# Gate/up products over three PSUM bank pairs, W_in loaded in two DMAs, and tile 1's transposes released per bank: a recurrent block with a gated MLP on eight Trainium2 cores

## The chip, the cores and the metric

The kernel runs on all 8 NeuronCores of one Trainium2 chip. The time of a run is the device time of the slowest core, in microseconds (us). The figure that is compared is the median of several runs. A profile is one more execution, recorded by the hardware profiler; its page shows the slowest core.

## What is computed

A layer norm feeds two branches: a linear recurrence along the sequence between two projections, and a gated MLP with integer weights scaled by 1/127. The result is x + s * silu(ffn).

```python
xn = layernorm(x)                       # x: (2, 16384, 1024) float32
# recurrent branch, on sequences of length 16384
gu = gamma * (xn @ W_in.T + b_in)
h[t] = lam * h[t-1] + gu[t]             # lam = exp(lambda_log), elementwise
s  = h @ W_out.T + b_out + xn
# gated MLP: DIM 1024, HIDDEN 3072, weights are int * (1/127)
g  = silu( (silu(xn @ wg.T) * (xn @ wu.T)) @ wd.T )
out = x + s * g
```

## The kernel before

Each core takes 4096 rows of one sequence (a quarter) in 8 tiles of 512 rows, numbered 1 to 8. Ahead of them stands tile 0, the 256 rows before the core's own, of which only the recurrence's state is wanted. The kernel is written for the five engines directly: `tensor_tile`, `scalar_tile`, `vector_tile`, `sync_tile` and `gpsimd_tile` each append one engine's instructions and waits for a tile, in the order in which that engine will run them. A wait (`W`) names a mark, and a mark is a semaphore's value once the operation (`O`) that carries it has ended. Nothing reorders: an engine that waits holds back all that stands behind it. DMAs issued by SyncE form the queue q1, those issued by GpSimd the queue q0.

TensorE runs these stages on a tile k:

- **T**: 8 blocks of 4 transposes (2 in tile 0) of the normalized rows `xnb` into PSUM banks 0 to 3, in turn (L245). Even blocks are copied to `xnbT` by ScalarE (L364), odd ones by VectorE (L418); the marks are `("Tevac", k, kc)`.
- **U**: 8 blocks of 8 matmuls with `winT` into banks 0 and 1 (L264). ScalarE scales them into `guT` (L379, marks `("guevac", k, ec)`), and VectorE scans them (L425).
- **gate/up**, not in tile 0: 24 blocks c of 8 gate matmuls (L287) and 8 up matmuls (L295). Their weights come in 12 groups of two blocks, 1 MB each, through two buffers `wgubuf`; SyncE reloads one (L504) when the up matmuls of the group two before are done. ScalarE applies SiLU to the gate bank (L390, marks `gsilu`), VectorE multiplies it with the up bank (L458, marks `gumul`) into `hbT`, and runs one scan after each third block. There are two `siluT` buffers.
- **S**: 8 blocks of one bias matmul (L310) and 8 matmuls with `woutT` (L315) into banks 0 and 1, evacuated by VectorE (L471).
- **down**: 4 row blocks m, in the order 1, 0, 2, 3, of 48 matmuls each with `wdfull` (L333), into banks 2m and 2m+1. ScalarE applies SiLU to each bank (L348, marks `("dsilu", k, b)`); for the banks 4 to 7 it does so after the next tile's T stage. GpSimd multiplies with s and adds x (L527, L531), and stores (L542).

In the gate/up stage a block uses two pairs of banks in turn:

```python
gb = 2 + 2 * (c % 2)
ub = 3 + 2 * (c % 2)
if c >= 2:
    W("tensor", mark=("gsilu", k, c - 2))
    W("tensor", mark=("gumul", k, c - 2))
```

At the start, SyncE issues x for tile 0 in two halves (L145), three small loads (eps, lambda, the identity) between them, x for tile 1 (2 MB, L139), five more small loads (gamma, b_in, b_out, mask, ones; L156), and then the first two `wgubuf` groups. GpSimd issues `winT` as one DMA that casts float32 to bf16 (L160), waits for it (L162), and then issues `woutT` (L165), the four parts of `wdfull` (L513) and x for tile 2 (L139). TensorE starts with two waits: for the three and for the five small loads (L169, L170). VectorE likewise waits for the five before it takes the statistics of tile 1 (L185), and ScalarE takes their square root (L210) before it evacuates tile 0's transposes. ScalarE normalizes tile 1 (L226) between those evacuations and the first evacuation of tile 0's U stage.

Of the kernel before, what the change touches and what calls it, by code (L numbers as in the profile page):

```python
# [63 lines left out]
def build_nc():  # L64
# [65 lines left out]
    def walk():  # L130
# [23 lines left out]
        for src, dst in ((gam_h, gam_sb), (bin_h, bin_sb), (bout_h, bout_sb),  # L154
                         (mask_h, mask_sb), (ones_h, ones_sb)):
            O("sync", lambda eng, s=src, d=dst: eng.dma_start(d[:, :], s[:, :]),  # L156
              inc="s_sets", n=16)
        src_w = win_t.rearrange("(kc p) e -> p kc e", p=128)
        dst_w = winT[:, :].rearrange("p (kc e) -> p kc e", e=D)
        O("gpsimd", lambda eng, s=src_w, d=dst_w: eng.dma_start(d, s),  # L160
          inc="s_setg", n=16, mark=("wcast", 0))
        W("gpsimd", mark=("wcast", 0))  # L162
        src_w2 = wout_t.rearrange("(kc p) e -> p kc e", p=128)
        dst_w2 = woutT[:, :].rearrange("p (kc e) -> p kc e", e=D)
        O("gpsimd", lambda eng, s=src_w2, d=dst_w2: eng.dma_start(d, s),  # L165
          inc="s_setg", n=16, mark=("wcast", 1))


# [64 lines left out]
        def tensor_tile(k):  # L233
            real = k >= 1
            W("tensor", mark=("LN", k))
            if k == 1:
                W("tensor", mark=("guevac", 0, 7))
            jw = 2 if k == 0 else 4
            for kc in range(NK):
                if kc >= 4:  # L240
                    W("tensor", mark=("Tevac", k, kc - 4))
                elif k >= 2:
                    W("tensor", mark=("dsilu", k - 1, kc))
                for j in range(jw):
                    O("tensor", lambda eng, kc=kc, j=j: eng.transpose(  # L245
                        pb[kc % 4][:, j * 128:(j + 1) * 128],
                        xnb[:, j * D + kc * 128: j * D + kc * 128 + 128],
                        ident_sb[:, :]),
                        inc=None if j < jw - 1 else "s_t",
                        mark=None if j < jw - 1 else ("T", k, kc))  # L250
            if k == 0:
                W("tensor", mark=("wcast", 0))
            for ec in range(NK):
# [7 lines left out]
                for kc in range(NK):  # L261
                    if ec == 0:
                        W("tensor", mark=("Tevac", k, kc))
                    O("tensor", lambda eng, ec=ec, kc=kc, tw=tw: eng.matmul(  # L264
                        pb[ec % 2][:, 0:tw],
                        winT[:, kc * D + ec * 128: kc * D + ec * 128 + 128],
                        xnbT[:, kc * T: kc * T + tw],
                        start=(kc == 0), stop=(kc == NK - 1)),
                        inc=None if kc < NK - 1 else "s_t",
                        mark=None if kc < NK - 1 else ("U", k, ec))  # L270
            if not real:
                return
            for g in range(NGU):
                G = (k - 1) * NGU + g
                W("tensor", mark=("wgu", G))
                for cc in range(2):
                    c = 2 * g + cc
                    gb = 2 + 2 * (c % 2)
                    ub = 3 + 2 * (c % 2)
                    if c >= 2:  # L280
                        W("tensor", mark=("gsilu", k, c - 2))
                        W("tensor", mark=("gumul", k, c - 2))
                    elif k >= 2:
                        W("tensor", "s_a",
                          mark=("dsilu", k - 1, 3 if c == 0 else 5))
                    for kc in range(NK):
# [65 lines left out]
        def scalar_tile(k):  # L352
# [33 lines left out]
            for c in range(NHC):  # L386
                W("scalar", mark=("gmm", k, c))
                if c >= 2:
                    W("scalar", mark=("gumul", k, c - 2))
                O("scalar", lambda eng, c=c: eng.activation(  # L390
                    siluT[c % 2][:, :], pb[2 + 2 * (c % 2)][:, 0:512],
                    AF.Silu, scale=QINV),
# [8 lines left out]
        def vector_tile(k):  # L401
# [53 lines left out]
            for c in range(NHC):  # L455
                W("vector", mark=("umm", k, c))
                W("vector", mark=("gsilu", k, c))
                O("vector", lambda eng, c=c: eng.scalar_tensor_tensor(  # L458
                    hbT[:, c * T:(c + 1) * T], pb[3 + 2 * (c % 2)][:, 0:512],
                    QINV, siluT[c % 2][:, :], ALU.mult, ALU.mult),  # L460
# [205 lines left out]
```

How the kernel before makes its waits and increments, by code:

```python
    def play(eng, name):  # L575
        for item in sc.ops[name]:
            if item[0] == "op":
                _, make, inc, n = item
                ins = make(eng)
                if inc is not None:
                    ins.then_inc(sems[inc], n)
            else:
                _, sem, v = item
                eng.wait_ge(sems[sem], v)
```

## Time and profile before

| | |
|---|---|
| median of 2 runs | 1372.91 us (1371.90 to 1373.91) |
| the profiled execution | 1371.94 us |
| its span on core 0, the slowest | 1370.4 us |
| spans of all cores | 1355.9 to 1370.4 us |
| TensorE matmul busy on core 0 | 1294.2 us, 94% |
| VectorE, ScalarE, GpSimd busy | 347.0, 289.9, 198.9 us |
| DMA | 190.90 MB |
| granted TensorE clock | 0.992 to 0.995 |

The span runs from the first to the last instruction of a core. Busy times are sums over instructions; a TensorE that is 94% busy has few gaps, so what matters is where these gaps lie and what ends them. All times below count from the start of core 0's span.

### The profile page before, as it was taken

What the parts mean: (1) busy time and instruction counts of PE and PEld (TensorE: products, weight loads), DVE (VectorE), ACT (ScalarE), POOL (GpSimd) and SP (SyncE); (2) the same over time, 40 slices, a digit from 0 to 9 for tenths busy, and PEclk for the clock granted to TensorE, in tenths of its full rate; (3) what the DMA queues carried; (4) which work ended last, traced back from release to release, by engine and by line L of the source; (5) the groups of instructions that cost most, each with busy time, mean ns of one, the idle gap of its engine ahead of it and who ended that gap; (6) DMA issues with size and microseconds to landing.
All of it is one profiled execution on the core that took longest, in us unless ns stands there. A gap on an engine that the chain in (4) does not pass through costs nothing.

```text
span 1370.4 us, 15875 instructions; the slowest of 8 cores (1355.9 to 1370.4 us)
## 1 busy us (share of the span) xinstructions
PE 1294.2 (94%) x6032; PEld 588.9 (43%) x6032; DVE 347.0 (25%) x566; ACT 289.9 (21%) x437; POOL 198.9 (15%) x197
## 2 busy tenths in 40 slices
PE   0699999999998999989999899999999999999997
PEld 0444445444453445434454344544445444454443
DVE  1423321223112240123301233022320334012322
ACT  2521123110231112311222112221123110231100
POOL 0000021300312003210042001330031300331002
PEclk9999999999999999999999999999999999999999
DMA  9954405753067410865127640366306652065301
GB/s 209 249 159 154 123 16 176 220 173 93 31 215 219 150 62 31 261 200 153 32 62 248 203 150 14 112 229 213 123 19 189 220 160 90 31 220 178 124 1 62
DMA packets 124782, 190.90 MB, mean 139 GB/s; under 512 B 3491, under 2 KB 101923, under 8 KB 124708
## 3 DMA queue, kind: packets, MB, share of 16 engines
q1 hardware_dynamic: 101524, 103.90, 24.5%
q0 software_dynamic: 23184, 85.99, 20.2%
q8 instruction: 50, 0.82, 0.2%
q14 instruction: 24, 0.20, 0.1%
HBM read 177.29 MB, written 16.78 MB: 142 GB/s over the span
## 4 chain that ended last, share of the span: by engine, by line
PE 87%; DMA 10%; issue 1%; DVE 1%; ACT 0%; SPq 0%; ACTq 0%; DVEq 0%; POOL 0%; POOLq 0%
PE pb L333 24%; PE pb L287 21%; PE pb L295 21%; PE pb L315 9%; PE pb L264 9%; DMA wgubuf<-wgu_t 8%; PE pb L245 2%; DMA ones_sb<-ones 2%; PE pb L310 1%; DVE stats L185 0%; ACT xnb L226 0%; SPq L156 0%; ACT guT L379 0%; DVE xbuf L486 0%; ACT L230 0%
## 5 line engine op out<-in xcount | busy, mean ns | idle before, releaser
L287 PE MATMUL pb<-xnbT,wgubuf 128*128 128x512 bf16 x1536 | 367.0, 383 | 24.9 <-DMA wgubuf<-wgu_t 23.1
L295 PE MATMUL pb<-xnbT,wgubuf 128*128 128x512 bf16 x1536 | 363.7, 380 | 0.0
L333 PE MATMUL pb<-wdfull,hbT 128*128 128x512 bf16 x1536 | 332.8, 379 | 0.0
L458 DVE SCALAR_TENSOR_TENSOR hbT<-pb,siluT 128x512 bf16<-128x512 f32 x192 | 132.8, 692 | 597.7 <-PE pb L295 597.7
L287 PEld LDWEIGHTS pb<-xnbT,wgubuf 128*128 128x128 bf16 x1536 | 149.0, 98 | 214.4 <-issue 41.1
L390 ACT ACTIVATE siluT<-pb 128x512 bf16<-128x512 f32 x192 | 114.6, 597 | 567.3 <-PE pb L287 561.1
L295 PEld LDWEIGHTS pb<-xnbT,wgubuf 128*128 128x128 bf16 x1536 | 150.5, 98 | 182.8 <-issue 2.6
L333 PEld LDWEIGHTS pb<-wdfull,hbT 128*128 128x128 bf16 x1536 | 150.1, 98 | 181.4
L527 POOL TENSOR_TENSOR gslab<-gslab,s_sb 128x512 bf16<-128x512 bf16 x60 | 70.9, 1181 | 812.5 <-ACT gslab L348 805.4
L264 PE MATMUL pb<-xnbT,winT 128*128 128x512 bf16 (+1 forms) x576 | 122.1, 374 | 4.0 <-ACT guT L379 4.0
L315 PE MATMUL pb<-woutT,guT 128*128 128x512 bf16 x512 | 121.6, 381 | 0.0
L531 POOL TENSOR_TENSOR xbuf<-xbuf,gslab 128x512 f32<-128x512 f32 x60 | 74.8, 1247 | 180.0 <-issue 176.0
L264 PEld LDWEIGHTS pb<-xnbT,winT 128*128 128x128 bf16 x576 | 57.5, 100 | 65.4 <-issue 4.7
L418 DVE CAST xnbT<-pb 128x512 bf16<-128x512 f32 (+1 forms) x36 | 23.6, 662 | 242.9 <-PE pb L245 242.7
L425 DVE TENSOR_TENSOR_SCAN guT<-lam_sb,carry,guT 128x512 bf16<-128x512 f32 x64 | 82.7, 1292 | 0.0
L245 PE MATMUL pb<-ident_sb,xnb 128*128 128x128 f32 x272 | 33.8, 282 | 39.4 <-DMA ones_sb<-ones 32.5
L315 PEld LDWEIGHTS pb<-woutT,guT 128*128 128x128 bf16 x512 | 44.8, 98 | 59.9 <-issue 14.5
L379 ACT ACTIVATE guT<-pb,bgam_sb,gam_sb 128x512 bf16<-128x512 f32 (+1 forms) x72 | 54.4, 756 | 57.1 <-PE pb L264 57.1
L471 DVE TENSOR_TENSOR s_sb<-pb,xnb 128x512 bf16<-128x512 f32 x64 | 44.3, 692 | 87.5 <-PE pb L315 87.5
L348 ACT ACTIVATE gslab<-pb 128x512 bf16<-128x512 f32 x64 | 33.9, 601 | 91.4 <-PE pb L333 66.3
L210 ACT ACT_TABLE_LOAD x9 | 11.5, 1283 | 194.9 <-DVE mv L190 194.9
L364 ACT CAST xnbT<-pb 128x512 bf16<-128x512 f32 (+1 forms) x36 | 20.1, 561 | 149.9 <-PE pb L245 149.9
(29 smaller groups left out, 242.4 us busy)
## 6 DMA issues: line engine op xcount, KB each, us to landing
wgubuf<-wgu_t SPq DMA_DIRECT2D x96, 1024.0 KB, 5.8
wdfull<-wd_t POOLq DMA_DIRECT2D x32, 1536.0 KB, 18.7
out<-xbuf POOLq DMA_DIRECT2D x32, 512.0 KB, 3.0
xbuf<-xe POOLq DMA_DIRECT2D x7, 2048.0 KB, 13.1
winT<-win_t POOLq DMA_DIRECT2D x1, 2048.0 KB, 30.3
xbuf<-xe SPq DMA_DIRECT2D x1, 2048.0 KB, 26.0
woutT<-wout_t POOLq DMA_DIRECT2D x1, 2048.0 KB, 18.8
xbuf<-xe SPq DMA_DIRECT2D x2, 512.0 KB, 8.6
```

The lines of the kernel that those rows point to most:

```text
L245: O("tensor", lambda eng, kc=kc, j=j: eng.transpose(pb[kc % 4][:, j * 128:(j + 1) * 128], xnb[:, j * D + kc * 128: j * D + kc * 128 + 128] ...
L264: O("tensor", lambda eng, ec=ec, kc=kc, tw=tw: eng.matmul(pb[ec % 2][:, 0:tw], winT[:, kc * D + ec * 128: kc * D + ec * 128 + 128], xnbT[: ...
L287: O("tensor", lambda eng, g=g, cc=cc, kc=kc, gb=gb: eng.matmul(pb[gb][:, 0:512], wgubuf[g % 2][:, kc * 512 + cc * 128: kc * 512 + cc * 128 ...
L295: O("tensor", lambda eng, g=g, cc=cc, kc=kc, ub=ub: eng.matmul(pb[ub][:, 0:512], wgubuf[g % 2][:, kc * 512 + 256 + cc * 128: kc * 512 + 25 ...
L315: O("tensor", lambda eng, b=b, m=m, n=n, kc=kc: eng.matmul(pb[b % 2][:, 0:512], hTb[:, kc * T + m * 128: kc * T + m * 128 + 128], woutT[:, ...
L333: O("tensor", lambda eng, c=c, m=m, n=n: eng.matmul(pb[2 * m + n][:, 0:512], hbT[:, c * T + m * 128: c * T + m * 128 + 128], wdfull[:, c * ...
L379: O("scalar", lambda eng, ec=ec, tw=tw: eng.activation(guT[:, ec * T: ec * T + tw], pb[ec % 2][:, 0:tw], AF.Identity, bias=bgam_sb[:, ec:e ...
L390: O("scalar", lambda eng, c=c: eng.activation(siluT[c % 2][:, :], pb[2 + 2 * (c % 2)][:, 0:512], AF.Silu, scale=QINV), inc="s_a", mark=("g ...
L425: eng.tensor_tensor_scan(hTb[:, ec * T: ec * T + tw], lam_sb[:, ec:ec + 1].broadcast_to([128, tw]), guT[:, ec * T: ec * T + tw], init, ALU ...
L458: O("vector", lambda eng, c=c: eng.scalar_tensor_tensor(hbT[:, c * T:(c + 1) * T], pb[3 + 2 * (c % 2)][:, 0:512], QINV, siluT[c % 2][:, :] ...
L527: O("gpsimd", lambda eng, b=b, m=m, n=n: eng.tensor_mul(gslab[b % 4][:, :], gslab[b % 4][:, :], s_sb[:, m * D + n * 512: m * D + n * 512 + ...
L531: O("gpsimd", lambda eng, b=b, m=m, n=n, p=p: eng.tensor_add(xbuf[p][:, m * D + n * 512: m * D + n * 512 + 512], xbuf[p][:, m * D + n * 51 ...
```

## The change

In words: `winT` comes in two DMAs of four k-blocks each, and GpSimd waits for each before it issues the next; TensorE waits for a half when the first U block of tile 0 reaches it, instead of for all of it before the stage. TensorE's wait ahead of tile 1's transposes for the last evacuation of tile 0 becomes two waits, one per bank. The gate/up blocks use three pairs of banks (2 to 7) in turn instead of two (2 to 5), and wait for block c - 3 instead of c - 2; the third block of a tile waits for the SiLU of the last down bank of the tile before.

```diff
--- before.py
+++ after.py
@@ -155,15 +155,19 @@
                          (mask_h, mask_sb), (ones_h, ones_sb)):
             O("sync", lambda eng, s=src, d=dst: eng.dma_start(d[:, :], s[:, :]),
               inc="s_sets", n=16)
-        src_w = win_t.rearrange("(kc p) e -> p kc e", p=128)
-        dst_w = winT[:, :].rearrange("p (kc e) -> p kc e", e=D)
-        O("gpsimd", lambda eng, s=src_w, d=dst_w: eng.dma_start(d, s),
-          inc="s_setg", n=16, mark=("wcast", 0))
-        W("gpsimd", mark=("wcast", 0))
+        for h in range(2):
+            src_w = win_t[h * 512:(h + 1) * 512, :].rearrange(
+                "(kc p) e -> p kc e", p=128)
+            dst_w = winT[:, h * 4 * D:(h + 1) * 4 * D].rearrange(
+                "p (kc e) -> p kc e", e=D)
+            O("gpsimd", lambda eng, s=src_w, d=dst_w: eng.dma_start(d, s),
+              inc="s_setg", n=16, mark=("winh", h))
+            W("gpsimd", mark=("winh", h))
         src_w2 = wout_t.rearrange("(kc p) e -> p kc e", p=128)
         dst_w2 = woutT[:, :].rearrange("p (kc e) -> p kc e", e=D)
         O("gpsimd", lambda eng, s=src_w2, d=dst_w2: eng.dma_start(d, s),
           inc="s_setg", n=16, mark=("wcast", 1))
+
 
 
         W("tensor", "s_seta", value=NSETUP_A)
@@ -233,14 +237,14 @@
         def tensor_tile(k):
             real = k >= 1
             W("tensor", mark=("LN", k))
-            if k == 1:
-                W("tensor", mark=("guevac", 0, 7))
             jw = 2 if k == 0 else 4
             for kc in range(NK):
                 if kc >= 4:
                     W("tensor", mark=("Tevac", k, kc - 4))
                 elif k >= 2:
                     W("tensor", mark=("dsilu", k - 1, kc))
+                elif k == 1 and kc < 2:
+                    W("tensor", mark=("guevac", 0, 6 + kc))
                 for j in range(jw):
                     O("tensor", lambda eng, kc=kc, j=j: eng.transpose(
                         pb[kc % 4][:, j * 128:(j + 1) * 128],
@@ -248,8 +252,6 @@
                         ident_sb[:, :]),
                         inc=None if j < jw - 1 else "s_t",
                         mark=None if j < jw - 1 else ("T", k, kc))
-            if k == 0:
-                W("tensor", mark=("wcast", 0))
             for ec in range(NK):
                 if ec == 0:
                     W("tensor", mark=("Tevac", k, 4))
@@ -261,6 +263,8 @@
                 for kc in range(NK):
                     if ec == 0:
                         W("tensor", mark=("Tevac", k, kc))
+                        if k == 0:
+                            W("tensor", mark=("winh", kc // 4))
                     O("tensor", lambda eng, ec=ec, kc=kc, tw=tw: eng.matmul(
                         pb[ec % 2][:, 0:tw],
                         winT[:, kc * D + ec * 128: kc * D + ec * 128 + 128],
@@ -275,14 +279,14 @@
                 W("tensor", mark=("wgu", G))
                 for cc in range(2):
                     c = 2 * g + cc
-                    gb = 2 + 2 * (c % 2)
-                    ub = 3 + 2 * (c % 2)
-                    if c >= 2:
-                        W("tensor", mark=("gsilu", k, c - 2))
-                        W("tensor", mark=("gumul", k, c - 2))
+                    gb = 2 + 2 * (c % 3)
+                    ub = 3 + 2 * (c % 3)
+                    if c >= 3:
+                        W("tensor", mark=("gsilu", k, c - 3))
+                        W("tensor", mark=("gumul", k, c - 3))
                     elif k >= 2:
                         W("tensor", "s_a",
-                          mark=("dsilu", k - 1, 3 if c == 0 else 5))
+                          mark=("dsilu", k - 1, 3 + 2 * c))
                     for kc in range(NK):
                         O("tensor", lambda eng, g=g, cc=cc, kc=kc, gb=gb: eng.matmul(
                             pb[gb][:, 0:512],
@@ -388,7 +392,7 @@
                 if c >= 2:
                     W("scalar", mark=("gumul", k, c - 2))
                 O("scalar", lambda eng, c=c: eng.activation(
-                    siluT[c % 2][:, :], pb[2 + 2 * (c % 2)][:, 0:512],
+                    siluT[c % 2][:, :], pb[2 + 2 * (c % 3)][:, 0:512],
                     AF.Silu, scale=QINV),
                     inc="s_a", mark=("gsilu", k, c))
             if k < NT:
@@ -456,7 +460,7 @@
                 W("vector", mark=("umm", k, c))
                 W("vector", mark=("gsilu", k, c))
                 O("vector", lambda eng, c=c: eng.scalar_tensor_tensor(
-                    hbT[:, c * T:(c + 1) * T], pb[3 + 2 * (c % 2)][:, 0:512],
+                    hbT[:, c * T:(c + 1) * T], pb[3 + 2 * (c % 3)][:, 0:512],
                     QINV, siluT[c % 2][:, :], ALU.mult, ALU.mult),
                     inc="s_v", mark=("gumul", k, c))
                 if c % 3 == 1:
```

## Rows read from the trace of the kernel before

**Rows 1.** Cores: span and mean granted clock.
```profile
core 0: 1370.4 us, clock 0.993
...
core 6: 1366.6 us, clock 0.992
```
**Rows 2.** Waits of TensorE, core 0: line, releaser: total us, times, longest us.
```profile
PE pb L245 <- DMA ones_sb<-ones: 32.5, 1, 32.5
PE pb L287 <- DMA wgubuf<-wgu_t: 23.1, 17, 2.8
PE pb L245 <- ACT xnbT L364: 5.8, 1, 5.8
PE pb L264 <- ACT guT L379: 4.0, 2, 3.7
PE pb L287 <- DVE hbT L458: 0.9, 1, 0.9
```
**Rows 3.** Timeline, 16 to 33 us: start, us, what, count [idle before <-releaser].
```profile
16.00 1.29 DVE L185 BATCH_NORM_STATS2 stats<-xbuf 128x6 f32<-128x512 f32 x2 [9.36 <-DMA xbuf<-xe]
...
32.36 0.17 DVE L406 TENSOR_TENSOR bgam_sb<-bin_sb,gam_sb 128x8 f32<-128x8 f32 x1 [12.51 <-DMA ones_sb<-ones]
32.44 0.89 POOL L165 DMA_DIRECT2D woutT<-wout_t  x1 [29.81 <-DMA winT<-win_t]
```
**Rows 4.** Timeline, 42 to 62 us.
```profile
42.19 3.34 PE L264 MATMUL pb<-xnbT,winT 128*128 128x256 bf16 x16
...
49.24 5.92 PE L264 MATMUL pb<-xnbT,winT 128*128 128x256 bf16 x40 [3.71 <-ACT guT L379]
...
57.24 2.38 PE L245 MATMUL pb<-ident_sb,xnb 128*128 128x128 f32 x20 [0.81 <-ACT guT L379]
...
59.10 1.29 DVE L418 CAST xnbT<-pb 128x512 bf16<-128x512 f32 x2 [0.21 <-issue]
...
59.94 1.50 PE L245 MATMUL pb<-ident_sb,xnb 128*128 128x128 f32 x12 [0.32 <-DVE xnbT L418]
```
**Rows 5.** DMA queues (packets, MB, share): 0:16.5, 5:9, 14:25, 29.5:32, 35:36, 37:47 us.
```profile
q0 software_dynamic: 544, 1.11, 54.9%
...
q0 software_dynamic: 203, 0.42, 91.5%
...
q0 software_dynamic: 421, 0.86, 52.5%
q1 hardware_dynamic: 421, 1.70, 48.6%
...
q0 software_dynamic: 10, 0.01, 3.2%
...
q0 software_dynamic: 11, 0.02, 38.8%
...
q0 software_dynamic: 760, 1.56, 107.1%
```
**Rows 6.** DMA queues, 765:769 us, and the matmuls that waited (timeline).
```profile
q0 software_dynamic: 284, 1.16, 100.6%
...
775.73 3.47 PE L287 MATMUL pb<-xnbT,wgubuf 128*128 128x512 bf16 x8 [2.79 <-DMA wgubuf<-wgu_t]
```
**Rows 7.** Issue of x(2) (timeline); DMA issues, us to landing; first use of woutT.
```profile
36.60 0.79 POOL L139 DMA_DIRECT2D xbuf<-xe  x1
...
xbuf<-xe POOLq DMA_DIRECT2D x1, 2048.0 KB, 40.4
...
159.39 1.90 PE L315 MATMUL pb<-woutT,guT 128*128 128x512 bf16 x8
```
**Rows 8.** Timeline, tile 3: a product and the bank wait put down to it.
```profile
431.97 0.69 DVE L458 SCALAR_TENSOR_TENSOR hbT<-pb,siluT 128x512 bf16<-128x512 f32 x1 [1.57 <-PE pb L295]
...
436.13 1.89 PE L287 MATMUL pb<-xnbT,wgubuf 128*128 128x512 bf16 x8 [0.89 <-DVE hbT L458]
```
**Rows 9.** Timeline of ScalarE, tile 2: SiLU of the last four down banks.
```profile
221.41 2.07 ACT L348 ACTIVATE gslab<-pb 128x512 bf16<-128x512 f32 x4
```

## The prediction

> **What bounds the kernel now.** I read the cores first: the slowest, core 0, spans 1370.4 us, core 6 is next at 1366.6 [rows 1]. The profiled run took 1371.94 us, so 1.54 us lie around the span; the median of the two timed runs is 1372.91, 0.97 above it. My sum is made against 1371.94 and moved by +0.97 at the end.
>
> TensorE's waits come next [rows 2], since TensorE is busy for 94% of the span. Three parts count: 32.5 us before its first instruction, put down to the DMA of ones_sb; 5.8 and 4.0 us on ScalarE in the prologue; and 23.1 us in 17 waits for wgubuf reloads. One single wait, 0.9 us, is put down to the VectorE product that frees a gate/up bank. Whatever the change gives has to come from the prologue or from one of these named waits.
>
> The prologue is a chain behind one event. At 32.3 us the last small constant lands; VectorE goes on at 32.36 [rows 3], TensorE at 32.5. VectorE then does the statistics for tile 1, ScalarE waits for them before it evacuates tile 0's transposes (the 5.8 us), and TensorE reaches the first winT matmul at 42.19 [rows 4]. winT had landed when GpSimd went on, at 32.44 [rows 3], nearly 10 us before: the old wait for all of winT costs nothing.
>
> **Part 1, winT in two DMAs, with finer waits on TensorE.** By itself the finer wait is worth nothing, for the reason just given. What can move is when the constants land, because they share the DMA engines with winT. The two landings coincide within 0.1 us [rows 3], and from 29.5 to 32 us the queue of winT, q0, has only 10 packets left at 3.2% of 16 engines, about half of one engine [rows 5]: one last engine, shared by both queues, ends both.
>
> Now the split. q0 had moved 544 of winT's 1024 packets by 16.5 us; between 14 and 25 us it moved 421, or 38 per us [rows 5]. So half of winT (512) is moved at 16.5 - 32/38 = 15.7 us on average. The whole would be through at 16.5 + 480/38 = 29.1, while the last engine ends at 32.3, some 3 us late; half of that late at half way puts the landing of the first half at about 17.2. GpSimd sees it and issues the second. The nearest row for the hole that opens in q0 is woutT: issued at 32.44 [rows 3], its first 11 packets in 35 to 36 us at 38.8% [rows 5], so about 2.9 us from issue to packets. The second half starts at about 20.1.
>
> On the last engine, 17.2 to 32.3 are 15.1 us, half of them (7.5) for each queue. In the hole q1 has the engine alone and does 2.9 of its 7.5 us; 4.6 are left at 20.1, with 7.5 of q0.
> - If both then share equally, q1 ends after 9.2 us, at 29.3 to 29.4: the chain starts 2.9 us earlier. That is the good end.
> - If q0 first keeps the engine for itself for more than 2.9 us, all of winT is again moved before the constants; the engine's work is the same as before and they land at 32.3: gain 0.
>
> Which? Two rows speak for the second. When winT started, q0 had 91.5% of the engines from 5 to 9 us [rows 5], although x0's second half had been issued before, at 2.92; its statistics could start only at 16.00 [rows 3]. And from 765 to 769 us an x load of q0 had 100.6% while a wgubuf reload was pending, for which TensorE waited until 775.73 [rows 6]. By 9 us some 16 packets for each of 16 engines were through (203, and a few before 5 us) [rows 5]. 16 of the 32 that an engine has in a half cost 16/32 x 7.5 = 3.8 us on the last engine, more than 2.9. So I take a point near the zero end, **0.5 us saved**, for holds that turn out shorter. Both ends, 0 and 2.9, stay in the range.
>
> On who gets an engine the Trainium skill ("DMA: Bandwidth & Descriptors", section Queues, rings and completion order) says that each DMA engine turns to the next queue only after a whole packet of some 9 to 17 descriptors, at most 64. The trace agrees at the starts of q0's transfers (91.5% and 100.6%); by that rule the gain is the same 0 that the rows gave.
>
> The other effects of the split are covered. At the good end the second half has 7.5 - 4.6 = 2.9 us of work left at 29.3 and shares with wgubuf, so it lands at 35.1; it is first needed after the transposes, at 42.19 - 2.9 = 39.3: 4.2 us of cover. And the tile-0 projection stops after two blocks for 3.71 us until ScalarE comes back from tile 1's layer norm (49.24) [rows 4], so only a landing after about 43 costs anything, one for one from there. Queued behind GpSimd's two waits are woutT, four wdfull loads and last x(2), all later by at most 2.9 us. The last, x(2), landed at 36.6 + 40.4 = 77.0; woutT is first read at 159.39, and wdfull and x(2) after that [rows 7]: 79 us of cover at least. SyncE's queue waits for none of it.
>
> **Part 2, tile 1's first transposes.** Before, they wait for the last evacuation of tile 0 (0.81 us idle before 57.24) [rows 4]. After, block 0 can start when the projection ends, about 56.45, and block 1 waits for that last evacuation. But block 5 needs bank 1 back from VectorE, whose copy stands behind the last scan, the 8 carry copies and the mask product, and starts at 59.10 whatever TensorE does; TensorE waits for it before 59.94 [rows 4]. So the 0.8 us turn into a longer wait there: **0**, at most 0.8 if VectorE were not late.
>
> **Part 3, three pairs of gate/up banks.** The only bank wait on core 0 is 0.9 us before 436.13. The product that frees that bank (block 8, freeing it for block 10) ran from 431.97 for 0.69 us, so it had been done for 3.5 us [rows 8]. Block 10 is the first of a group, and what really came last was its wgubuf load, which a third pair doesn't touch. Normally the 8 matmuls of a half block take at most 1.89 us [rows 8], so a block between leaves over 3 us for a product of 0.69 (2.0 with a scan ahead): two pairs suffice. **0**, at most 0.9. The new wait, of block 2 for the SiLU of the last down bank, is covered: on tile 2 that group of four ran from 221.41 for 2.07 us [rows 9], ahead of every evacuation of U on the same engine, and U's 64 matmuls stand between them and the gate/up stage. siluT still has two buffers, so ScalarE's and VectorE's own waits stay.
>
> **Sum.** 1371.94 - 0.5 + 0 + 0 = 1371.4 on the profiled run's scale, 1372.4 on that of the median.
>
> **The rivals.**
> - *Equal sharing* of the second half with q1: 1372.9 - 2.9 = 1370.0. For it: 421 against 421 packets from 14 to 25 us [rows 5]. Against it: the first 5 us of winT and the x load at 765. Chance 0.27.
> - *A slow start of the second half* (the other side). From 5 to 9 us q0 moved 203 packets at 91.5%, 55 per us of a full share, while woutT alone moved 760 in 10 us at 107.1%, 71 [rows 5]. If each start of such a transfer has its first 256 packets at the slower rate, that is 256/55 - 256/71 = 1.1 us more engine work ahead of the constants; it decides once q0 also keeps the engines for over 2.9 us. Time 1372.9 + 1.1 = 1374.0. Against it: the x load's start moved 284 packets in 4 us, 71 per us [rows 6]. Chance 0.13.
> - *The wgubuf waits fall otherwise.* Core 0 waits 23.1 us for them [rows 2]. If a small shift re-deals how reloads meet x loads and stores, core 0 could lose up to the distance to the next core, 3.8 us [rows 1]: 1369.1; or some core could gain as much. Chance 0.10 for both together.
> - *The change removes waits of its own*: earlier transposes and the third pair give both their bounds, 0.8 + 0.9 = 1.7 us: 1371.2. [rows 4, 8] speak against both. Chance 0.05.
> - The forecast, 1372.4: chance 0.45.
>
> For one DMA more, the same page of the Trainium skill (section Anatomy of one DMA) gives a fixed cost of about 2.0 us; the hole read from woutT is 2.9 us from issue to first packet. With 2.0 the equal-sharing rival would be worth an estimated 2.0 us.
>
> **How the numbers follow.** The low end is equal sharing plus both bounds of parts 2 and 3, 1370.0 - 0.8 - 0.9 = 1368.3, less 1.0 for half the spread of the two timed runs: 1367.3. The high end is the slow start, 1374.0, plus 2.5, most of the 3.8 us by which a core could gain wgubuf waits: 1376.5. A change of over 2%, about what a measurement of this kernel can tell, is 27 us. No case here comes near it: winT's second half would have to land 27 us after 43, or more than all wgubuf waits (23.1) to vanish. Faster 0.01, within 2% 0.98, slower 0.01.
>
> **What would show it.** Right: TensorE's first wait still 31.5 to 32.5 us on core 0; q1's share falling under 20% for some us after about 20; the transposes of tile 1 starting earlier, but its projection at the old distance from the first instruction; the wgubuf waits as long as before in sum, with a bank wait now and then still named at the first block of a group. Equal sharing: first wait near 29.6. Wrong in its ground: a wait of TensorE on winT's second half, or gaps inside a wgubuf group that were there before and are gone.

## The result

The changed kernel takes 1364.32 us (median of 32 runs) against 1373.38 us (31 runs of the kernel before beside it). The ratio is 0.9936, 95% interval 0.9920 to 0.9953: 8.8 us faster, 0.64%, within 2%. The forecast was 1372.4 us with a range down to 1367.3, so the time lies 3 us below the range. It moved the way that was forecast, but by 9 us instead of 0.5. The ratios, and the mean spans below, are taken over the executions in which neither die ran at a lowered clock.

The profiled execution took 1361.88 us, 10 us less than the one of before. First two rows of the view of its cores (span, mean granted clock):

```profile
core 0: 1354.7 us, clock 0.994
...
core 6: 1360.4 us, clock 0.993
```

Then its page (of core 6, the slowest), the engines' busy time and the DMA issues (op, count, KB each, median us to landing):

```profile
PE 1293.2 (95%) x6032; PEld 590.3 (43%) x6032; DVE 347.9 (26%) x566; ACT 290.0 (21%) x437; POOL 197.0 (14%) x198
...
winT<-win_t POOLq DMA_DIRECT2D x2, 1024.0 KB, 16.1
xbuf<-xe SPq DMA_DIRECT2D x1, 2048.0 KB, 20.2
```

TensorE is as busy as before (1294.2 us then). The load of tile 1's x by SyncE takes 20.2 us to land; on the page of before it was 26.0. Now TensorE's waits on core 0 (line, releaser: total us, times, longest us), to be held against [rows 2]:

```profile
PE pb L249 <- DMA ones_sb<-ones: 23.7, 1, 23.7
PE pb L291 <- DMA wgubuf<-wgu_t: 16.4, 9, 3.8
PE pb L249 <- ACT xnbT L368: 5.8, 1, 5.8
PE pb L268 <- ACT guT L383: 3.6, 2, 3.4
...
PE pb L291 <- DVE hbT L462: 0.9, 1, 0.9
```

The first wait has gone from 32.5 to 23.7 us. It is the same on every core: 30.0 to 33.2 us before, 23.3 to 25.2 after. The other two waits of the prologue in the list, for ScalarE (ACT), are as long as they were, within 0.4 us. The following table holds means over the 8 cores, from the same two profiles; the first gate/up block is where the prologue ends for this purpose.

| mean over the cores, us | before | after |
|---|---|---|
| TensorE's first instruction | 31.52 | 23.98 |
| from there to tile 1's projection | 29.47 | 29.45 |
| start of the first gate/up block | 74.75 | 67.20 |
| from there to the end of the span | 1288.1 | 1287.6 |
| span | 1362.9 | 1354.8 |

7.5 of the 8.1 us in the mean span are gained before TensorE's first instruction. The timeline of the start on core 0 shows what was released when (start us, us, engine, line, what [idle before <-releaser]):

```profile
17.74 0.76 POOL L163 DMA_DIRECT2D winT<-win_t  x1 [15.26 <-DMA winT<-win_t]
...
23.54 0.17 DVE L410 TENSOR_TENSOR bgam_sb<-bin_sb,gam_sb 128x8 f32<-128x8 f32 x1 [4.59 <-DMA ones_sb<-ones]
...
33.36 3.62 PE L268 MATMUL pb<-xnbT,winT 128*128 128x256 bf16 x16
...
33.67 0.88 POOL L168 DMA_DIRECT2D woutT<-wout_t  x1 [15.18 <-DMA winT<-win_t]
```

GpSimd goes on behind the first half of winT at 17.7 us, the constants are in at 23.5 (before: 32.3, [rows 3]), and GpSimd goes on behind the second half at 33.7. By the trace the halves had landed some 0.5 us before that, at 17.2 and 33.1. And the DMA queues of the same core, in the stretches 5:9, 16:22, 22:23, 23:24 and 24:29 us (packets, MB, share of 16 engines):

```profile
q0 software_dynamic: 218, 0.45, 96.9%
q1 hardware_dynamic: 90, 0.04, 6.5%
...
q1 hardware_dynamic: 758, 1.72, 96.9%
q0 software_dynamic: 8, 0.01, 1.0%
...
q1 hardware_dynamic: 407, 0.25, 81.5%
q0 software_dynamic: 22, 0.05, 28.1%
...
q0 software_dynamic: 63, 0.13, 73.7%
q1 hardware_dynamic: 105, 0.11, 34.9%
...
q0 software_dynamic: 316, 0.65, 80.6%
q1 hardware_dynamic: 313, 0.32, 25.6%
```

Up to 9 us it is the picture of before [rows 5]. Then, from 16 to 22 us, q1 has 97% of the engines where it had about half. It puts x(1) and the small loads through in that time. The second half of winT was issued at 17.74, but its first packet comes at 21.95; from 23 us on it takes 74 to 81% of the engines, and by 23.5 the constants are in. From the landing of the first half to that packet are 4.8 us, where the forecast had 2.9, and q0 as a whole moves only 8 packets in the 6 us from 16 to 22.

### The profile page after: what moved, and what is told of

It is laid out like the page before. It is cut to its first block, busy times and chain, and to the rows that moved or that the text cites. A ratio compares the mean times of both kernels' runs of the same rounds, so it can differ in the third digit from the quotient of the medians.

```text
span 1360.4 us, 15876 instructions; the slowest of 8 cores (1345.2 to 1360.4 us)
## 1 busy us (share of the span) xinstructions
PE 1293.2 (95%) x6032; PEld 590.3 (43%) x6032; DVE 347.9 (26%) x566; ACT 290.0 (21%) x437; POOL 197.0 (14%) x198
## 4 chain that ended last, share of the span: by engine, by line
PE 90%; DMA 7%; DVE 1%; issue 1%; ACT 0%; SPq 0%; ACTq 0%; DVEq 0%; POOL 0%; POOLq 0%
PE pb L337 24%; PE pb L291 23%; PE pb L299 22%; PE pb L268 9%; PE pb L319 9%; DMA wgubuf<-wgu_t 5%; PE pb L249 2%; PE pb L314 1%; DMA ones_sb<-ones 1%; DVE stats L189 0%; SPq L156 0%; ACT xnb L230 0%; DVE hbT L462 0%; ACT guT L383 0%; DVE xbuf L490 0%
## 5 line engine op out<-in xcount | busy, mean ns | idle before, releaser
L291 PE MATMUL pb<-xnbT,wgubuf 128*128 128x512 bf16 x1536 | 365.8, 381 | 23.9 <-DMA wgubuf<-wgu_t 18.3
L422 DVE CAST xnbT<-pb 128x512 bf16<-128x512 f32 (+1 forms) x36 | 23.6, 661 | 242.9 <-PE pb L249 242.6
L249 PE MATMUL pb<-ident_sb,xnb 128*128 128x128 f32 x272 | 33.9, 282 | 31.3 <-DMA ones_sb<-ones 24.4
L368 ACT CAST xnbT<-pb 128x512 bf16<-128x512 f32 (+1 forms) x36 | 20.1, 562 | 150.0 <-PE pb L249 150.0
## 6 DMA issues: line engine op xcount, KB each, us to landing
xbuf<-xe SPq DMA_DIRECT2D x1, 2048.0 KB, 20.2
```

What stands on the lines that cost most here:

```text
L249: O("tensor", lambda eng, kc=kc, j=j: eng.transpose(pb[kc % 4][:, j * 128:(j + 1) * 128], xnb[:, j * D + kc * 128: j * D + kc * 128 + 128] ...
L291: O("tensor", lambda eng, g=g, cc=cc, kc=kc, gb=gb: eng.matmul(pb[gb][:, 0:512], wgubuf[g % 2][:, kc * 512 + cc * 128: kc * 512 + cc * 128 ...
```

## The experiments

The kernels e1 to e4 ran on one chip, e5 to e8 on a second, e9 to e12 on a third and e13 to e16 on a fourth, each group beside the kernel before on the same chip. The slowest of eight cores scatters by some 4 us from run to run, so beside the ratio I give the mean span over the cores, in the mean over the runs, as the difference from the kernel before, with its standard error (se); and from each kernel's profile TensorE's first instruction and the first gate/up block, in the mean over the cores. Only the second and the third chip have a profile of the unchanged kernel beside the others (e5, e10).

| kernel | ratio, 95% interval | mean span, against before, us | first instr. | first gate/up |
|---|---|---|---|---|
| winT split only (e1) | 0.9958 (0.9932 to 0.9984) | -7.0 (se 0.9) | 23.9 | 67.1 |
| the two other parts (e2) | 0.9983 (0.9956 to 1.0010) | -2.3 (0.7) | 30.7 | 73.8 |
| both halves at once (e3) | 0.9965 (0.9943 to 0.9986) | -2.5 (0.8) | 30.6 | 73.5 |
| small loads first (e4) | 0.9988 (0.9959 to 1.0017) | -0.6 (0.8) | 27.9 | 73.0 |
| before, control (e5) | 1.0002 (0.9973 to 1.0031) | +0.3 (1.1) | 31.2 | 74.6 |
| the changed kernel again (e6) | 0.9956 (0.9930 to 0.9982) | -7.7 (0.7) | 24.0 | 67.4 |
| winT late (e7) | 0.9969 (0.9941 to 0.9996) | -6.7 (0.8) | 22.0 | 64.9 |
| late, small loads first (e8) | 0.9988 (0.9949 to 1.0026) | -5.4 (1.2) | 16.6 | 62.4 |
| three bank pairs only (e9) | 0.9981 (0.9955 to 1.0007) | -1.5 (0.9) | 31.2 | 74.5 |
| before, control (e10) | 0.9987 (0.9957 to 1.0018) | -0.6 (1.1) | 30.7 | 74.2 |
| x in four DMAs (e11) | 0.9851 (0.9819 to 0.9884) | -16.4 (0.7) | 24.0 | 67.5 |
| transposes only (e12) | 0.9992 (0.9971 to 1.0014) | +0.1 (0.7) | 31.0 | 74.1 |
| as e11, two bank pairs (e13) | 0.9842 (0.9814 to 0.9869) | -18.1 (1.1) | 24.8 | 68.3 |
| e11 again (e14) | 0.9844 (0.9817 to 0.9871) | -16.8 (0.8) | 24.9 | 68.4 |
| second half held (e15) | 0.9950 (0.9925 to 0.9975) | -4.9 (0.9) | 24.3 | 67.2 |
| x in two DMAs (e16) | 0.9840 (0.9807 to 0.9873) | -18.2 (0.8) | 24.1 | 67.4 |

The theory after the comparison of the traces (A): all of the gain is the earlier landing of the constants, and it comes from the hole in q0. The rivals: (B, later C) the bank rotation and the transposes carry a part of it; (A2) the smaller transfers do it, not the hole.

**e1: only the split.** The edit, on the kernel before:

```diff
-        O("gpsimd", <winT in one DMA>, mark=("wcast", 0))
-        W("gpsimd", mark=("wcast", 0))
+        for h in range(2):
+            O("gpsimd", <four k-blocks of winT>, mark=("winh", h))
+            W("gpsimd", mark=("winh", h))
...
-            if k == 0:
-                W("tensor", mark=("wcast", 0))
+                        if k == 0:
+                            W("tensor", mark=("winh", kc // 4))
```

> The kernel before with only the split of winT (two DMAs, GpSimd waits for each) and the finer wait of TensorE. Theory A (all of the gain is the earlier landing of the constants, which in the profile of the changed kernel came at 23.3 to 25.2 us against 30.0 to 33.2): TensorE's first wait 23 to 25 us on every core, time about 8 to 9 us under the kernel before, ratio 0.9935. Theory B (the bank rotation or tile 1's transposes carry a part): ratio nearer to 1, 0.995 to 0.998, and the rest shows in the run with the other two parts.

The first gate/up block starts at 67.1 us, as in the changed kernel, and the mean span is 7.0 us shorter against 7.7 with all parts (e6, on another chip); the standard error of the difference is 1.1. So the split alone carries the gain, as far as that error lets one tell. The ratio, 0.9958, is not the 0.9935 that theory A gave and would by itself have spoken for B; but the whole change has 0.9956 in e6. Against the expectation, one core had its constants at 27.3 us instead of 23 to 25; the others had 22.5 to 24.1. On core 1 the second half was issued at 17.27 and its packets ran from 22 us, on core 0 it was issued at 19.19. The DMA queues of this kernel in 22:23 us (packets, MB, share), first core 1, then core 0:

```profile
q0 software_dynamic: 56, 0.11, 78.0%
q1 hardware_dynamic: 196, 0.12, 41.3%
...
q1 hardware_dynamic: 400, 0.37, 106.3%
q0 software_dynamic: 3, 0.01, 3.4%
```

And TensorE's first wait (total us, times, longest us) on core 1 and on core 0:

```profile
PE pb L248 <- DMA ones_sb<-ones: 27.3, 1, 27.3
...
PE pb L248 <- DMA ones_sb<-ones: 24.1, 1, 24.1
```

On core 1 q0 took 78% of the engines before the constants were in, and they came 3.2 us later than on core 0. I read it as a race between the end of the hole and the last small load, which the last small load usually wins by little: of the 56 cores in the seven profiles with this hole, 4 had the constants at 27.3 to 28.6 us. It isn't the issue time alone that decides: core 3 of e1 issued its second half at 16.68, before core 1, and had its constants at 22.5.

**e2: only the other two parts.** The changed kernel with winT as one DMA and the one wait for it ahead of the projection.

> The kernel before with only the three bank pairs and the two finer waits ahead of tile 1's transposes; winT stays one DMA. Theory A: no gain, ratio 1.000 within 0.002; the projection of tile 1 starts at the old distance (28.8 us on core 0) from TensorE's first instruction. Theory B: 1 to 4 us gained, ratio 0.997 to 0.999, and gaps at the third to last blocks of a tile that are gone.

First instruction and first gate/up block are where the controls have them, within 1 us. The ratio's interval holds 1.000; the mean span is 2.3 us shorter, three standard errors, which theory A did not expect. The timed runs alone leave the rotation open here; the traces settle its mechanism, as e13 shows below.

**e3: split without a hole.** The changed kernel, both halves issued back to back:

```diff
             O("gpsimd", lambda eng, s=src_w, d=dst_w: eng.dma_start(d, s),
-              inc="s_setg", n=16, mark=("winh", h))
-            W("gpsimd", mark=("winh", h))
+              inc="s_setg" if h == 0 else "s_wh1", n=16, mark=("winh", h))
+        W("gpsimd", mark=("winh", 0))
+        W("gpsimd", mark=("winh", 1))
```

> The changed kernel, but GpSimd issues both halves of winT back to back (each on a semaphore of its own) and waits for both only before woutT; so the transfer is split but q0 is never empty. Theory A1 (the gain is the hole in q0 between the halves, in which q1 has all engines): constants land at 30 to 33 us again, ratio about 1.000. Theory A2 (the gain comes from the smaller transfers themselves): constants at 23 to 25 us, ratio 0.9935.

The DMA queues of core 0 in 16:22 us:

```profile
q1 hardware_dynamic: 240, 0.98, 50.9%
q0 software_dynamic: 238, 0.47, 50.5%
```

TensorE's first wait there:

```profile
PE pb L250 <- DMA ones_sb<-ones: 31.2, 1, 31.2
```

Half and half again, and the constants at 31.2 (29.8 to 31.2 over the cores). So it is the hole, not the size of the transfers: A2 has fallen. The timed ratio of 0.9965, with an interval that doesn't hold 1.000, was not expected; the first gate/up block is at most 1.1 us earlier than in the two controls, and the 2.5 us in the mean span are those of e2, on the same chip.

**e4: the small loads first.** One edit on the kernel before: the five small loads are issued ahead of x0's second half and of x(1).

> The kernel before with one edit: SyncE issues the five small loads ahead of x0's second half and of tile 1's x. If it is only the constants that are late (they stand last in q1), TensorE's first wait ends when tile 0's rows are normalized, at 22 to 24 us, but VectorE's statistics of tile 1 still need x(1), which landed at 29.4 us before; then the projection of tile 1 starts 2 to 3 us earlier than before, ratio 0.998. If x(1) didn't matter the gain would be the full 8 us.

TensorE started at 27.9 us, later than expected, because x0's second half, now behind the small loads, was in at 21.8 us on core 0 instead of 16.0 [rows 3]. The first gate/up block came 1.3 to 1.6 us earlier than in the two controls (on other chips), against 2 to 3 expected: VectorE's statistics of tile 1 had to wait for x(1) until 30.85 us on core 0, so x(1) is nearly as late as the constants. Bringing in one item of q1 earlier is worth little; all of q1 has to come in earlier.

**e5 and e6: the kernel before and the changed kernel, on one chip.**

> The kernel before, unchanged, as a control with a profile from the same chip as the changed kernel beside it. Ratio 1.000; first wait of TensorE 30 to 33 us; how far the part after the first gate/up block (span minus its start, mean 1288.1 us over the cores before) and the timed ratio move without any edit is what the other runs have to be read against. If the third bank pair is worth nothing, this part is the same here as in the changed kernel on the same chip, within 1 us in the mean over cores; if it is worth something, 1 to 4 us longer.

> The changed kernel, unchanged, on the same chip as the control. Ratio 0.9935 to 0.995; first wait 23 to 25 us; first gate/up block 7.5 us earlier than in the control in the mean over the cores; the part after it the same.

7.1 us between the two first gate/up blocks, 7.7 us (se 0.7) in the mean span. From the first gate/up block on, the two profiles have 1289.4 and 1289.5 us in the mean over the cores: the rest of the change adds nothing there that one profile of each could show.

**e7: no split, winT late.**

```diff
+        W("gpsimd", mark=("x", 0))
         src_w = win_t.rearrange("(kc p) e -> p kc e", p=128)
```

> The kernel before with one edit: GpSimd waits for x0's second half before it issues winT, still as one DMA. No split. If what counts is that q1 has the engines alone for some us before the constants, it works as well as the split: constants at 20 to 26 us, winT landing at about 30, in time for the projection at constants + 9.7 us, first gate/up block 6 to 9 us earlier than in the control, ratio 0.993 to 0.996. If the split itself is needed: constants at 30 to 33 us.

The timeline of core 0:

```profile
9.12 1.04 POOL L161 DMA_DIRECT2D winT<-win_t  x1 [8.42 <-DMA xbuf<-xe]
...
20.69 1.94 PE L246 MATMUL pb<-ident_sb,xnb 128*128 128x128 f32 x8 [20.69 <-DMA ones_sb<-ones]
...
33.78 2.51 PE L265 MATMUL pb<-xnbT,winT 128*128 128x256 bf16 x11 [3.20 <-DMA winT<-win_t]
```

And its DMA queues in 16:22 us:

```profile
q0 software_dynamic: 397, 0.81, 83.0%
q1 hardware_dynamic: 408, 0.38, 25.1%
```

One DMA, and the constants at 17.1 to 25.2 us, the first gate/up block 9.7 us before the control's. The split isn't needed; what is needed is that q1 goes first. winT becomes the next limit: TensorE waits 3.2 us for it. In the timed runs only 6.7 us (se 0.8) of the 9.7 arrive. In the profiles the mean span is 8.3 us under the control's (1355.7 against 1363.9), and TensorE's waits for wgubuf are 2.5 us longer in the mean over the cores (19.7 against 17.2), which covers the part lost there; why the timed runs lose more stays open.

**e8: the changed kernel with winT late, both halves at once, and the small loads first.**

> The changed kernel with three edits of its start: the five small loads ahead of x0's second half, GpSimd waits for x0's second half before winT, and both halves of winT are then issued together. If x(1)'s landing is the next thing that sets the chain (as when only the small loads were moved), it now lands at 18 to 23 us because q1 goes first; TensorE's first instruction at 14 to 18 us, the projection of tile 1 at 48 to 51 us against 53.4 in the changed kernel, ratio 0.990 to 0.993. If winT is late instead, TensorE waits for it and the projection of tile 1 comes no earlier than 53.

The prologue came out as expected (TensorE from 16.6 us, tile 1's projection at 48.6), and both named limits are there: on core 0 TensorE first waits for tile 0's normalized rows, and later 5.7 us for winT's second half. Its waits:

```profile
PE pb L251 <- ACT xnb L232: 16.0, 1, 16.0
...
PE pb L270 <- DMA winT<-win_t: 5.7, 1, 5.7
```

The ratio is a miss: 12.2 us earlier at the first gate/up block against the control, but 5.4 us (se 1.2) in the mean span of the timed runs, from only 6 runs. Its own profile is 11.3 us under the control's in the mean span (1352.7 against 1363.9), so the two measures disagree; where the rest goes wasn't found.

**e9, e10, e12: the small parts one by one, with a control.** e9 has only the rotation (`c % 3`, waits for c - 3), e12 only the waits ahead of tile 1's transposes.

> The kernel before with only the rotation over three bank pairs. What is open: with both small parts in and winT whole, the mean span over the cores was 2.3 us (standard error 0.7) under that of the kernel before in the timed runs, while the profiles put nothing there. Theory A (the rotation is worth nothing): mean span as the control's within 1.5 us. Theory C (it is worth about 2 us in small amounts that single profiles don't resolve): 1.5 to 3 us shorter, and the part after the first gate/up block shorter than the control's by that.

> The kernel before, unchanged: the profile of the same chip against which the banks-only and transposes-only runs are read. Ratio 1.000 within 0.003; mean span within 1.5 us of the other runs of it; first gate/up block at 74 to 75.5 us in the mean over the cores.

> The kernel before with only the two finer waits ahead of tile 1's transposes. Theory A: nothing; the first four transposes run about 0.8 us earlier, TensorE waits longer for VectorE's copy instead, the projection of tile 1 starts 29.0 to 30.0 us after TensorE's first instruction as before; mean span within 1.5 us of the control's. If the 0.8 us came through, the projection would start at 28.2 to 29.0.

The transposes bring nothing that shows: +0.1 us (se 0.7), and the projection 29.4 us after TensorE's first instruction, as before. The rotation alone gave -1.5 us (se 0.9), beside a control of the unchanged kernel with -0.6 (1.1): not told apart. The other sign of theory C, a shorter part after the first gate/up block, is not there: 1286.1 us with three pairs, 1282.5 in the control.

**e11, e14, e16: the lesson applied to x.** On the changed kernel, GpSimd loads x for tile k+2 in parts, each waited for:

```diff
+        def x_load_parts(k):
+            for j in range(4):
+                r0 = WARM + (k - 1) * T + j * 128
+                src = xe[r0:r0 + 128, :]
+                dst = xbuf[k % 2][:, j * D:(j + 1) * D]
+                mk = ("x", k) if j == 3 else ("xp", k, j)
+                O("gpsimd", lambda eng, s=src, d=dst: eng.dma_start(d, s),
+                  inc=f"s_x{k % 2}", n=16, mark=mk)
+                if j < 3:
+                    W("gpsimd", mark=mk)
...
-                x_load(k + 2)
+                x_load_parts(k + 2)
```

> The changed kernel with one edit: GpSimd loads x for tile k+2 in four DMAs of 512 KB, each waited for before the next, instead of one of 2 MB. It carries the lesson of the winT split over: a long transfer on q0 keeps q1 out, holes let q1 in. If this holds for the wgubuf reloads (waits of TensorE 16 to 17 us in the mean over the cores, up to 2.8 to 5.6 us each, the longest beside x loads), these waits fall to 8 to 12 us and the mean span is 5 to 8 us under that of the changed kernel, ratio 0.988 to 0.991. If the reloads are late for another reason (stores, the neighbour core's traffic): no change from the changed kernel, 0.9935 to 0.996.

> The kernel with winT split, three pairs and x in four DMAs, again, for the comparison on one chip. Ratio 0.983 to 0.988; wgubuf waits of TensorE 7 to 10 us in the mean over the cores.

> As x in four DMAs, but in two of 1 MB each, the second after the first has landed. If it is the length of the turn on q0 that holds the wgubuf reloads up, one hole instead of three helps in part: wgubuf waits of TensorE 10 to 14 us in the mean over the cores, between 8.4 (four) and 16 to 17 (one), and a ratio between 0.986 and 0.993. If any split does it: as with four.

TensorE's waits for wgubuf in the mean over the cores: 16.3 and 17.3 us in the two profiles of the changed kernel, 8.4 and 6.0 with x in four, 6.0 with x in two. On core 0, the slowest of e11's profile:

```profile
PE pb L302 <- DMA wgubuf<-wgu_t: 12.4, 11, 3.6
```

The ratio, 0.9851 (0.9819 to 0.9884), is better than expected. It beats both kernels: 1.5% or 20 us less than before, where the changed kernel has 0.4 to 0.6%. In the mean span it is 16.4 us against the 7.7 of e6. Two DMAs do it as well as four (0.9840), so the dose that e16's expectation named isn't there.

The traces show why one hole is enough. From 100 us on, and over all cores, 44 of the 721 reloads of the changed kernel were issued just before q0 took 80% or more of the engines for 3 us; they took 8.6 us to land in the median, where the 613 beside an idle q0 (under 10%) took 5.4. In before it is 45 of 728, with 9.1 against 5.4. With x in four (e11, e14, and e13 with two bank pairs) and with x in two (e16) not one reload met such a stretch, and 1 to 3 took over 9 us where 18 did in the changed kernel. This is the version to keep.

**e13: two bank pairs beside three, with the smaller waits.**

> The kernel with winT split and x in four DMAs, but with two gate/up bank pairs again. Beside the same kernel with three pairs it isolates the rotation where the wgubuf waits scatter less. Theory A (rotation worth nothing): mean span over the cores as with three pairs within 1 us (it was 1344.0). Theory C (worth about 2 us): 1.5 to 3 us longer than with three pairs.

With two pairs the mean span is 1341.9 us (se 1.0, 6 runs), with three 1343.2 (0.6, 4 runs). Theory C wanted the two pairs 1.5 to 3 us longer; they are 1.3 us shorter, with a standard error of 1.2. The times alone would still let the rotation be worth up to about 1 us.

The traces say more. In the profiles of the six kernels with two pairs (before, e1, e5, e10, e12, e13), over all cores and tiles, TensorE has no gap above 0.15 us before any odd block; each gap at the start of a block stands before an even one, the first of a group, where it also waits for wgubuf. And the product of block c - 2 had always ended at least 2.07 us before block c started. So no block ever waited for the product that frees its bank, and a third pair had nothing to take away: theory C has fallen. The -2.3 and -2.5 us of e2 and e3 stay without an explanation, but they are not bank waits.

**e15: the second half held back.**

```diff
+            if h == 1:
+                W("gpsimd", "s_sets", value=NSETUP_S)
```

> The changed kernel with one wait more: GpSimd issues the second half of winT only when the five small loads have landed. If the hole in q0 is what brings the constants in, a hole that can't end too early gives 22 to 24.5 us on every core (in the split-only run one core, whose second half came early, had 27.3), and q1's share stays near 100% until they are in. The second half then lands at 36 to 38 us, about 3 us later than in the changed kernel, and TensorE waits for it: the projection of tile 1 comes 0 to 2 us later than in the changed kernel, since 3.4 to 4.6 us of waiting for ScalarE stand behind the first two blocks. If the constants came from something else, their landing stays spread as before.

The constants came at 23.6 to 24.8 us on all eight cores, where e13 and e14 each had one or two cores at 27.9 to 28.6. With 4 late cores in 56 elsewhere, eight without one would be no surprise by luck either. What the run does show is that all of q1's loads up to the constants fit into the hole when it is held open. The DMA queues of core 0 in 17:24.5 us:

```profile
q1 hardware_dynamic: 1903, 2.37, 102.4%
q0 software_dynamic: 2, 0.00, 0.0%
```

GpSimd issued the second half at 24.60 us there, and the queues of the 3 us that followed, 24.6:27.6, are these:

```profile
q1 hardware_dynamic: 767, 0.77, 77.2%
q0 software_dynamic: 20, 0.04, 25.0%
```

TensorE's two DMA waits of the start on core 0:

```profile
PE pb L251 <- DMA ones_sb<-ones: 24.3, 1, 24.3
...
PE pb L270 <- DMA winT<-win_t: 1.3, 1, 1.3
```

TensorE now waits 0.2 to 1.4 us for winT's second half, but tile 1's projection starts at 53.45 us, as in the changed kernel (53.44): the wait for ScalarE behind the first two blocks takes it up. The expected loss of up to 2 us didn't come in the prologue. The timed mean span, though, gains 4.9 us (se 0.9), less than the 7.7 (0.7) of the changed kernel on another chip; the profile has no row for that difference.

## Why the prediction was wrong

- **Where the time is.** Right: the prologue behind the constants, and only it. The projection of tile 1 keeps its distance from TensorE's first instruction (29.45 against 29.47 us), and 7.5 of 8.1 us lie ahead of that instruction.
- **The first half's landing.** Right: forecast 17.2 us, landed at 17.2 on core 0, 15.6 us after its issue at 1.58. But the second half was issued at 17.74, and the sum had nothing for these 0.6 us.
- **The hole in q0: the step that failed.** "The second half starts at about 20.1." I took 2.9 us from woutT's issue to its packets [rows 3, 5] and let them begin at the landing. On core 0 the second half had its first packet at 21.95, 4.8 us after the landing: 0.6 until the issue and 4.2 from there. One row of one core was too little: from issue to the third packet woutT took 1.8 to 3.8 us over the eight cores of before, and the second half 3.6 to 4.9 over the 56 cores of the seven profiles with this hole. e7 has the like: winT was issued at 9.12, and in 10:14 q1 is alone:

```profile
q1 hardware_dynamic: 480, 1.10, 95.5%
```

- **The good end was no end.** I made "q1 alone in the hole, then shared or held" of it and bounded the gain by 2.9 us. q1 needed 6.3 us from the first half's landing (17.2 to 23.5), my sum had 7.5, and all but the last 1.5 us of it lay in the hole. What q0 does after the hole, on which the whole argument between the two rivals turned, comes nearly all after the constants. Where q0 does come back before them, as on core 1 of e1, the landing is at 27.3, between the usual 23.5 and the 29.3 that my sum had for equal sharing.
- **The hold by q0: not there.** The forecast of 0.5 rested on q0 keeping the engines for itself for more than 2.9 us when the second half starts. In 23:24 it moved 63 packets to q1's 105, in 24:29 316 to 313. Its share of 80.6% is no hold: packets pass one for one, and q0's take longer. [rows 6] was read the wrong way round. The wgubuf reload was issued at 764.6 us, when the x load, issued at 758.1, was already running; the reload was the late starter there, as the second half is here. In 5:9 too, winT had been issued first, at 1.58 against 2.92 for x0's second half. In before, a reload that started against q0 at 80% or more took 9.1 us to land in the median, beside an idle q0 5.4. So each queue starts late against the other's traffic, and these rows spoke for a longer hole, not for a hold. On who gets an engine the Trainium skill ("DMA: Bandwidth & Descriptors", section Queues, rings and completion order) has whole packets before each switch. The share at q0's first start fits (96.9% in 5:9), but at the second start no stretch shows a turn that keeps q1 out, and for the 4 us that q0 waits before it gets in the rule is no help.
- **The finer wait and its cover.** Right. Without it TensorE would have started the projection at most 0.3 us later on core 0 (GpSimd went on at 33.67, TensorE's first winT matmul ran at 33.36), under a wait of 3.4 us. The cover of 3.7 us that I had named is what e15 used up in part, at no cost.
- **Part 2, transposes.** Right, and as described. The changed kernel on core 0:

```profile
47.73 0.60 PE L249 MATMUL pb<-ident_sb,xnb 128*128 128x128 f32 x4
...
48.70 1.94 PE L249 MATMUL pb<-ident_sb,xnb 128*128 128x128 f32 x16 [0.37 <-ACT guT L383]
...
50.55 1.29 DVE L422 CAST xnbT<-pb 128x512 bf16<-128x512 f32 x2 [0.21 <-issue]
...
51.39 1.50 PE L249 MATMUL pb<-ident_sb,xnb 128*128 128x128 f32 x12 [0.76 <-DVE xnbT L422]
```

The first four transposes go ahead, and TensorE then waits 0.76 us for VectorE's copy where it waited 0.32 [rows 4]. With the wait for ScalarE ahead of it the sum is 1.13 us in both (0.37 + 0.76 now, 0.81 + 0.32 then). e12 measured +0.1 us (se 0.7).

- **Part 3, bank pairs.** Right: 0. No block ever waited for the product that frees its bank (e13), and the part after the first gate/up block is as long in e5 as in e6. The waits put down to hbT are still there with three pairs, 2.5 us in the mean over the cores against 1.9 before: they were never bank waits [rows 8].
- **The rival of the re-dealt wgubuf waits.** It played no part in the mean (17.0 us before, 16.4 after). But core 0, the slowest before, went from 23.1 to 16.4, and core 1 from 19.8 to 24.4; the 2 us by which the two profiled times differ beyond the mean span (10.1 against 8.1) can be such scatter.

## What to carry to other kernels

A small load that gates the start is as late as the whole queue that it stands in and the traffic beside it; ask which queue has the engines in each microsecond, and what it costs the other if the first leaves a hole. A large background transfer cut into two, with a wait between, lets the other queue through: here it brought 7.5 us at the start, and 9 to 10 us more in the mean span where x loads had stood in the way of weight reloads. When such a hole is priced, read its length off several cores and from landing to first packet, not off one row, and ask first whether the other queue finishes inside the hole. When two transfers meet, look which was issued first before calling one of them the holder.

## What the runs showed of the hardware

- With both queues full, equal numbers of packets pass, whatever their size: 421 and 421 of 2 and 4 KB before [rows 5], 316 and 313 of 2 and 1 KB after. So the share of the engines goes by packet cost: 80.6% to 25.6%.
- A transfer that starts against the other queue's traffic starts late, on either queue. On q0 the second half needed 3.6 to 4.9 us from issue to its third packet (56 cores), winT in e7 4.7 to 5.3 (8 cores). On q1 a reload of before lands 9.1 us after its issue in the median, instead of 5.4. How late it is isn't set by the other queue's share alone: in e15 the second half had its third packet 1.5 to 2.5 us after its issue, with q1 at 60 to 95% in the 3 us that followed. What decides was not found.
- q1 alone moves 758 packets (1.72 MB) in 16:22 us at 96.9%; with q0 beside it in e3, 240 (0.98 MB).
